# Transformer layer on one core: another order of TensorE's queue in the attention phase, with other PSUM banks, and the weights' rounding on two engines

## The reference

```python
x = x + attn(layernorm(x), w_q, w_k, w_v, w_o)
x = x + ffn(layernorm(x), w_gate, w_up, w_down, ...)
# attn: softmax(q k^T / sqrt(16)) v, per head, then w_o
# bitlinear(x, w): w_mean = mean(|w|)
#   w_q = clip(round(w / (w_mean + 1e-5)), -1, 1); x @ (w_q * w_mean * scale)^T
# ffn: int4_quant(x) -> gate, up by bitlinear; relu(gate)^2 * up -> int8_quant -> bitlinear(w_down)
```

## Time and profile before

| | us |
|---|---|
| median of 3 runs (1050.78 to 1052.41) | 1050.96 |
| the profiled execution | 1049.26 |
| its span, first to last instruction | 1046.9 |
| TensorE busy | 956.8 (91%) |
| VectorE busy | 839.2 (80%) |
| ScalarE busy | 764.9 (73%) |
| GpSimd busy | 274.3 (26%) |
| mean granted TensorE clock | 0.98 of full |

### The profile page before, as it was taken

The page is one execution under the profiler, slowest core; times in us unless marked ns, Lnnn a source line. Parts: engine busy times, 40 slices in busy tenths (PEclk is TensorE's granted clock), DMA queues, the critical chain, the costliest instruction groups (busy, mean ns, idle before and its releaser), DMA issues.

```text
span 1046.9 us, 16532 instructions
## 1 busy us (share of the span) xinstructions
PE 956.8 (91%) x5790; PEld 276.6 (26%) x5806; DVE 839.2 (80%) x1516; ACT 764.9 (73%) x1396; POOL 274.3 (26%) x321
## 2 busy tenths in 40 slices
PE   4799999999999999999989998899888998999997
PEld 3343222222222222222112221122111223444443
DVE  6597898888988888889878887789996245877774
ACT  5332788888888888898868887698886666776665
POOL 3500011101011010102991049601792220101110
PEclk9899999999999999999999999999999999999998
DMA  7300111121021123202122211141432002511000
GB/s 282 104 19 1 31 36 46 39 60 36 22 51 40 46 53 94 92 22 52 37 90 85 59 54 52 56 109 37 136 97 91 11 11 96 147 61 41 21 30 32
DMA packets 38040, 64.90 MB, mean 62 GB/s; under 512 B 3654, under 2 KB 19014, under 8 KB 37702
## 3 DMA queue, kind: packets, MB, share of 16 engines
q1 hardware_dynamic: 37958, 63.85, 20.8%
HBM read 42.27 MB, written 21.23 MB: 61 GB/s over the span
## 4 chain that ended last, share of the span: by engine, by line
PE 60%; POOL 10%; ACT 9%; DVE 9%; issue 8%; DMA 1%; SPq 1%; POOLq 0%; ACTq 0%; DVEq 0%
PE ps L429 16%; PE ps L373 12%; PE ps L351 7%; PE ps L408 7%; DVE mx L896 7%; PE ps L480 6%; PE ps L316 4%; PE ps L528 3%; PE ps L504 3%; POOL td L1154 2%; POOL tg L1154 2%; ACT PB L656 2%; POOL XV L1152 1%; ACT PB L738 1%; ACT nmT L667 1%
## 5 line engine op out<-in xcount | busy, mean ns | idle before, releaser
L896 DVE TENSOR_REDUCE mx<-ps 128x1 f32<-128x512 f32 x1024 | 643.7, 683 | 105.9 <-PE ps L373 105.6
L656 ACT ACTIVATE PB<-ps 128x512 f32<-128x512 f32 x1024 | 559.1, 596 | 135.9 <-PE ps L408 129.3
L373 PE MATMUL ps<-QK 48*128 48x512 f16 x1024 | 291.5, 387 | 31.5 <-DVE mx L896 25.8
L408 PE MATMUL ps<-QK 50*128 50x512 f16 x1024 | 291.6, 384 | 1.1 <-ACT XV L614 0.3
L429 PE MATMUL ps<-PB,Vg 128*32 128x512 f32 x2048 | 275.6, 611 | 0.0
L373 PEld LDWEIGHTS ps<-QK 48*128 48x128 f16 x1024 | 75.1, 93 | 370.1 <-DVE mx L896 296.3
L1129 POOL TENSOR_SCALAR nmb<-nm 128x16 f16<-128x16 f32 x32 | 6.5, 204 | 479.2 <-DVE nm L901 478.9
L351 PE MATMUL ps<-XV,wqk 128*128 128x512 f16 x384 | 112.2, 390 | 12.7 <-ACT nmT L667 12.0
L429 PEld LDWEIGHTS ps<-PB,Vg 128*32 128x32 f32 x2048 | 40.5, 108 | 109.0 <-ACT PB L656 78.8
L408 PEld LDWEIGHTS ps<-QK 50*128 50x128 f16 x1024 | 59.4, 94 | 34.9 <-ACT PB L656 20.2
L480 PE MATMUL ps<-wo,XV 128*128 128x512 f32 x128 | 61.0, 609 | 0.0
(11 more groups left out here) (128 smaller groups left out, 778.0 us busy)
## 6 DMA issues: line engine op xcount, KB each, us to landing
parts_d<-spl SPq DMA_DIRECT2D x64, 128.0 KB
att_d<-OS SPq DMA_DIRECT2D x32, 256.0 KB
QK<-parts_d SPq DMA_DIRECT2D x48, 128.0 KB, 4.7
QK<-parts_d SPq DMA_DIRECT2D x16, 256.0 KB, 4.6
XV<-att_d SPq DMA_DIRECT2D x2, 2048.0 KB, 9.9
QK<-rden_d SPq DMA_DIRECT2D x8, 512.0 KB, 6.8
wqk<-x SPq DMA_DIRECT2D x16, 256.0 KB, 3.8
out<-PB SPq DMA_DIRECT2D x16, 256.0 KB, 2.0
```

The lines of the kernel that those rows point to most:

```text
L373: nc.tensor.matmul(ps[:, at % S_BANKS, :], QK[rows, sup % 2, 2 * set_ + p, 0, half * HALF + qt * P:half * HALF + (qt + 1) * P], QK[rows, s ...
L408: nc.tensor.matmul(ps[:, T_BANK + n % T_BANKS, :], QK[rows, sup % 2, 2 * set_ + p, 1, kt * P:(kt + 1) * P], QK[rows, sup % 2, 2 * set_ + p ...
L656: nc.scalar.activation(PB[:, at % 3, 2 * (i % 2) + i // 2, :], ps[:, T_BANK + n % T_BANKS, :], ACT.Exp, scale=exp_reg).then_inc(probs, 1)
L896: nc.vector.tensor_reduce(mx[:, v % 2, idx, kh:kh + 1], ps[:, at % S_BANKS, :], AX.X, ALU.max).then_inc(s_used, 1)
```

## The change

Six edits, made together:

1. `pe_superunit` has an order of its own for each of the eight steps of a unit. The value sums of a step still come in the step after, but at another place in each. Pieces come as 0, 1, 2 + 1, 0, 3, 0, 2, 3 in steps 0 to 7.
2. Tiles lie on sides 0, 1, 0, 1.
3. Value sums always use bank 6, projection jobs in the loop bank 7. The first value sums of a unit wait for the copy of the sums of the unit before (`os_copy`); a job waits for the copy of the job before.
4. The maximum rows are written into the tiles' ring of three banks, in turn between the last tile of step 1 and the first of step 2 (33 places a unit).
5. On ScalarE the job's copy stands first in step 0, the sums' copy before exponential 3 of step 0, the rows' copy at the end of step 1; Abs in steps 4 and 6 (before 3 and 6). The matmul of a weight's mean moves from step 2 to the end of step 0 and VectorE's factor from step 3 to step 1.
6. Of the three GpSimd operations that make -1, 0, 1 the first, which rounds, stays; the other two give way to one `Sign` on ScalarE (bias -MAGIC), in steps 4 and 6 of the same units. A memset for the third weight moves from unit 23 to unit 24.

The diff, cut:

```diff
-MEAN_BANK = (7, 6, 7)
+MEAN_BANK = 7
+LATE = 1
+ROWS_AT = 1
+UNIT_TILES = 4 * KEYT + 1
...
+        def tile_place(at, r, i):
+            return UNIT_TILES * at + 4 * r + i + (1 if r > ROWS_AT else 0)
+        def rows_place(at):
+            return tile_place(at - 1, ROWS_AT, 3) + 1
+        def tile_bank_of(place):
+            return T_BANK + place % T_BANKS
...
         def pe_mean(pe, w):
             pe.wait_ge(w_tot, w + 1)
-            pe.wait_ge(rows_used, WEIGHT_MEANS[w] + 2)
+            pe.wait_ge(job_copy, WEIGHT_MEANS[w] + JOBS_AHEAD)
...
                 if n >= JOBS_AHEAD:
-                    pe.wait_ge(rows_used, n - JOBS_AHEAD + 2)
+                    pe.wait_ge(job_copy, n)
...
+        def pe_tile_free(pe, place):
+            taken = place - T_BANKS
+            if taken < 0:
+                return
+            at, k = taken // UNIT_TILES, taken % UNIT_TILES
+            rows = 4 * ROWS_AT + 4
+            if k == rows and at + 1 < UNITS:
+                pe.wait_ge(rows_used, at + 2)
+            else:
+                pe.wait_ge(probs, 4 * KEYT * at + k - (1 if k > rows else 0) + 1)
...
-            side, p = i // 2, i % 2
+            side, p = i % 2, i // 2
...
                 if at > 0:
-                    pe.wait_ge(rows_used, at + 1)
+                    pe.wait_ge(os_copy, at)
...
+                if r == 0:
+                    tile(0)
+                    tile(1)
+                    score(0)
+                    tile(2)
+                    score(1)
+                    score(2)
+                    values()
+                    score(3)
+                    tile(3)
+                    means()
...
+                elif r == 3:
+                    score(0)
+                    tile(0)
+                    tile(1)
+                    score(1)
+                    score(2)
+                    tile(2)
+                    values()
+                    score(3)
+                    tile(3)
...
+                elif r == 5:
+                    tile(0)
+                    score(0)
+                    score(1)
+                    tile(1)
+                    tile(2)
+                    score(2)
+                    values()
+                    tile(3)
+                    score(3)
...
+                elif r == 7:
+                    score(0)
+                    tile(0)
+                    tile(1)
+                    score(1)
+                    pieces(9, 12)
+                    tile(2)
+                    score(2)
+                    score(3)
+                    tile(3)
+                    values()
...
+        def act_ternary(act, w, q):
+            act.wait_ge(w_round[w], q + 1)
+            nc.scalar.activation(ternq(w, q), raw(w, q), ACT.Sign, bias=magic_neg[:]).then_inc(w_tern[w], 1)
...
+                if r == 0 and job_in(at - 1):
+                    act_job(act, job_in(at - 1))
                 act_exp(act, sup, step, 0)
                 act_exp(act, sup, step, 1)
-                if r == 0 and job_in(at - 1):
-                    act_job(act, job_in(at - 1))
-                if r == 1 and at > 0:
+                act_exp(act, sup, step, 2)
+                if r == 0 and at > 0:
                     act_sums(act, at - 1)
-                act_exp(act, sup, step, 2)
                 act_exp(act, sup, step, 3)
+                if r == 1 and at + 1 < UNITS:
+                    act_rows(act, at + 1)
-                if r in (3, 6):
+                if r in (4, 6):
...
-            nc.gpsimd.tensor_scalar(ternq(w, q), raw(w, q), MAGIC, 1.0, ALU.subtract, ALU.min).then_inc(w_min[w], 1)
-            own_wait(pool, w_min[w], q + 1)
-            nc.gpsimd.tensor_scalar(ternq(w, q), ternq(w, q), -1.0, 1.0, ALU.max, ALU.mult).then_inc(w_tern[w], 1)
```

More of the change, by code:

```diff
@@ L272, in job_bank @@
         def job_bank(n):
[L273 to L278, removed]
+            return AV_BANK + (n + 1) % 2 if n < JOBS_AHEAD else JOB_BANK
         def job_in(unit):
@@ L323, in pe_mean @@
             pe.wait_ge(w_tot, w + 1)
-            pe.wait_ge(rows_used, WEIGHT_MEANS[w] + 2)
-            nc.tensor.matmul(ps[:, MEAN_BANK[w], 8 * w:8 * w + 1], ones[:], wtot[:, w:w + 1], start=True, stop=True)\
+            pe.wait_ge(job_copy, WEIGHT_MEANS[w] + JOBS_AHEAD)
+            nc.tensor.matmul(ps[:, MEAN_BANK, 8 * w:8 * w + 1], ones[:], wtot[:, w:w + 1], start=True, stop=True)\
                 .then_inc(w_psum, 1)
@@ L397, in pe_scoresT @@
             set_, half = unit // 2, unit % 2
[L398 to L399 removed]
+            side, p = i % 2, i // 2
+            place = tile_place(sup * 4 + unit, kt, i)
             if kt == 0 and i == 0:
@@ L433, in pe_superunit, with score @@
         def pe_superunit(pe, sup, last):
[L435 to L438, removed]
             for step in range(STEPS):
                 at, r = sup * 4 + step // KEYT, step % KEYT
[L441 to L455, removed]
+                def score(j):
+                    ahead, unit, k = step_items(step)[j]
+                    if not (last and ahead):
+                        pe_scores(pe, sup + ahead, unit, k)
@@ new lines, in tile, with values, pieces, rows @@
+                def tile(i):
+                    pe_scoresT(pe, sup, step, i)
+                def values():
+                    if at * KEYT + r >= LATE:
+                        pe_av(pe, (at * KEYT + r - LATE) // STEPS, (at * KEYT + r - LATE) % STEPS)
+                def pieces(first, end):
+                    if job_in(at):
+                        for m in range(first, end):
+                            pe_job(pe, job_in(at), m)
+                def rows():
+                    if at + 1 < UNITS:
+                        pe_max_rows(pe, at + 1)
@@ L456, in pe_superunit @@
                 if last and step >= TAIL:
                     pe_attention_out(pe, (step - TAIL) // 2, range(step % 2 * 2, step % 2 * 2 + 2))
-                if r == 1 and at + 1 < UNITS:
-                    pe_max_rows(pe, at + 1)
-                if r == 2 and at in WEIGHT_MEANS:
-                    pe_mean(pe, WEIGHT_MEANS.index(at))
             if last:
-                pe_av(pe, sup, STEPS - 1)
+                for step in range(STEPS - LATE, STEPS):
+                    pe_av(pe, sup, step)
```

103 lines of the change are left out of this document (75 added, 28 removed).

## The result

The changed kernel takes **991.82 us** (990.27 to 992.04), against 1051.68 before on the same chips: a ratio of 0.9426, 95% interval 0.9409 to 0.9443. The forecast was 987, the range 970 to 1014. The profiled execution has a span of 988.5 us against 1046.9, so 58.4 us went, where the sum said 63.7.

The account below looks back on a forecast made before the run. About 2.6 of 22.58 us a unit were taken as queue order, not engine work. Gains 29.7 + 27.8 + 9.2 less 3.0 lost make 63.7 us; from the median 1050.96 this gives 987, range 970 to 1014.

Parts of the forecast that it names:

- What bounds the kernel: Ordinary units before the change: TensorE's own work is 19.96 of 22.58 us; about 2.6 us are queue order.
- The sum of slots: TensorE's own work in an ordinary unit of the new order: 19.78 us, plus 0.7 of waits.
- Ordinary units: Units 0 to 13: the walked new order takes 20.46 us instead of 22.58, 29.7 us gained.
- The first rival: Light steps stop at VectorE's limit or busy share bounds: 21.3 to 21.5 us a unit, 1012 us in all; chance 0.18.
- the slower one: Rival: value sums, their copy, exponential 3 and step 1's value sums chain beyond 2.26 us, up to 1068 us; chance 0.05.
- Weights: Units 14 to 25: GpSimd's stalls go, Abs, Sign and mean cost some; 262.3 us against 290.1, 27.8 gained.
- The Sign term: Units 14 to 25: two Signs cost 1.3 us a unit in four units, at 1.34 us per Sign, with some caught up later.
- Units 26 to 29: Units without pieces, VectorE the bound at 20.0 us; 85.5 us against 94.73, 9.2 gained.
- Signs in 27 and 28 fall mostly into TensorE's slack: 1.0 a unit: Units 27 and 28, without pieces: TensorE's slack mostly hides the Signs, leaving a cost of 1.0 us a unit.
- The two slow steps at the end: Last ruler interval, from unit 29 into step 2 of unit 30: two slow steps make it 22.3 us.
- Units 30 and 31: Units without scores, with output projection: 31.6 us a unit against 30.1, 3 us lost.
- 971: Rival: VectorE's 19.3 and TensorE's 19.8 reached, half of Abs and Sign hidden, 15 us more gained; chance 0.09.

Follow-up runs that it names:

- e1: The changed kernel with each step's queue order as in the kernel before; banks, sides, ScalarE's order and Sign stay as changed: 1022.26 us.
- e3: The changed kernel with the tiles back on sides 0, 0, 1, 1, its order kept: 1025.32 us.
- e4: The changed kernel with VectorE's maximum taken over only the first 256 of each 512 scores: 977.96 us.
- e8: The changed kernel with each Sign over only 16 columns of a quarter, the rest of the rounding to three values left out: 980.53 us.
- e5: The changed kernel with Abs and Sign moved from steps 4 and 6 to steps 2 and 4: 981.67 us.
- e7: The changed kernel with Abs and Sign in steps 2 and 4, and value sums ahead of tile 3 in units 30 and 31 (steps 2, 4, 7): 979.47 us.
- e9: e7 with the first projection piece of units 16 and 21 moved from step 1 to step 2: 978.22 us.

## Why the prediction was right, and where its terms were off

**What bounds the kernel.** Right. The queue's order was the loss: e1 gives 1.53 of the 2.14 us a unit back (with the new sides in place; e3 shows that the order needs them), and with VectorE's work halved (e4) a unit moves by 0.35 alone. The sum of slots, 19.78, was a floor that e4 with 20.09 came near.

**Ordinary units.** 20.46 walked, 20.44 measured, and each value sum within 0.06 us of its place. The first rival (slack not handed on, 21.3 to 21.5) did not happen; nor did the slower one, whose chain closed in the 2.28 us measured between the value sums of step 0 and 1, against 2.26 walked.

**Weights.** The waits ahead of the maximum rows went, as said. 27.8 forecast, 27.0 measured: two Abs cost 1.59 (said: 1.6), two Signs 1.59 (said: 1.3), the mean 0.9 (said: 1.0). The Sign term was short by 0.3 in each of four units. A Sign took 1.43 to 1.45 where the sum had 1.34, and of what was to be "caught up later" little was; the two shares were not told apart. How it looks in step 7 of unit 17 (TensorE's timeline; tile 3 behind the Sign of step 6):

```profile
480.20 0.39 PE L429 MATMUL ps<-QK 50*128 50x512 f16 x1 [0.70 <-ACT PB L773]
```

**Units 26 to 29.** The term that was mis-sized: 9.2 forecast, 3.7 measured after putting the mark right, which is about the whole miss of the sum (63.7 against 58.4). The largest step that failed reads "Signs in 27 and 28 fall mostly into TensorE's slack: 1.0 a unit". They cost 2.7 in unit 27 and 1.7 in unit 28 (23.54 and 23.71 against e8's 20.88 and 22.06), and more than that in unit 28, as said at e8. ScalarE's and TensorE's timelines there:

```profile
696.05 1.46 ACT L762 ACTIVATE td<-XV,magic_neg 128x1408 bf16<-128x1408 f32 x1
```

```profile
698.05 0.39 PE L429 MATMUL ps<-QK 50*128 50x512 f16 x1 [0.73 <-ACT PB L773]
698.37 1.07 PE L446 MATMUL ps<-PB,Vg 128*32 128x512 f32 x8
699.37 1.01 PE L429 MATMUL ps<-QK 50*128 50x512 f16 x3
...
700.74 1.93 PE L446 MATMUL ps<-PB,Vg 128*32 128x512 f32 x8
702.61 0.48 PE L385 MATMUL ps<-QK 48*128 48x512 f16 x1
```

TensorE waits 0.73 for the exponential behind the Sign, after having waited for VectorE just before; then the value sums take 1.93 us instead of 1.07. The windows above show the granted clock at 0.65 from 700 to 704, some of it at 1.2 GHz, behind a stretch (696 to 700) in which TensorE was busy 2.85 of 4 us. From 699.37 to 702.61 that is 3.24 us for the same matmuls that took 1.79 one unit earlier (677.79 to 679.58): 1.45 of the 2.7 go with the lower clock. I had read this fall of the clock in the earlier trace rows, as a cost that goes with GpSimd's stalls, and did not ask whether the change makes new idle time of the kind. In e5, with Signs elsewhere, unit 27 has 21.54. By these figures the Signs are 2.3 of the 5.5 us missed. The rest are smaller terms of the same sum. A unit with nothing but scores and tiles takes 20.23 (e8, from the value sums in step 1 of unit 27 to those in step 1 of unit 28) where 20.0 was said, a reduction being 0.61 and not 0.60: 0.9 in four units. The mean's matmul and factor cost 0.4 in unit 26 and were taken as nothing. VectorE's reciprocal, with the fall of the clock behind it in e8, cost 2.5 where 1.2 was said (20.88 + 22.06 against 2 x 20.23). The two slow steps at the end cost 2.9 where 2.3 was said (21.21, and the 1.9 by which the mark moved, against 20.23).

**Units 30 and 31.** Right: steps of 4.31 (said 4.35), 3.76 and 3.56 (3.54), and about 2.6 lost (3.0).

**The range.** It held easily: 991.8 lies near the forecast since the two large terms were right to 0.8 us. One of the rivals' sums is uneven: 971 is counted from 985.6 and the others from 987; from 987 it is 972.

## What to carry to other kernels

Where two or three engines hand small banks to each other, don't read the limit from busy shares. Sum the slots of each queue for one period, and walk the queue with start-to-start times and release times from the trace; if the walk repeats the present period to 0.01 us, it is worth trying on a new order of the same instructions (20.46 walked, 20.44 measured). It is only as good as its rules: for e3's sides the same walk said 2.1 where 1.25 was measured, since it let a matmul with a busy side hold up the next one. Then check separately the places where the period changes (no pieces, no scores, an extra operation of two slots on another engine), since the order tuned for the common period is not the best there: two such places were worth 12 us here.

## What the runs showed of the hardware that I had not expected

- Of two matmuls on different halves of the array's rows the later one in the queue can start first, when the earlier finds its half busy (e3: S0 at 396.70, T1, which stands before it, at 396.92; 1.25 us a unit, where the walk in strict order gave 2.1). Neither waited for a semaphore there, and what happens when one does this doesn't show. The Trainium skill (TensorE: Matmul & The Clock Gate, Part 3, "What overlaps and what doesn't") says that matmuls start and end in strict program order. This trace doesn't agree on the start: 0.22 us lie between the two, in the wrong order.
- Behind a stretch in which TensorE stalled for 0.73 us and several times for 0.2, the granted clock fell to its lower level (0.65 on average from 700 to 704 us), and that cost more (1.45 us) than the longest of the stalls. Where it falls changes with small shifts: e5, e7 and e9 have the same program in units 26 and 28, and the ruler reads 22.32, 22.28 and 20.78 in the one, 21.12, 21.12 and 23.82 in the other.
- A Sign over 128 x 1376 float32 took 1.43 to 1.45 us on ScalarE, a little more than an Abs (1.34 to 1.36), where GpSimd took 9.7 for the two operations that it replaced.
